# Causal attention of two heads side by side in blocks of 256 queries, with each block's division at a listed step

## What is computed

```python
q = einsum('bld,dhk->blhk', x, Wq)                # B, L, D, H, HD = 2, 2048, 256, 16, 64
latent = einsum('bld,dc->blc', x, Wkv_down)       # LD = 64
k = einsum('blc,chk->blhk', latent, Wk_up)
v = einsum('blc,chk->blhk', latent, Wv_up)
attn = einsum('bqhd,bkhd->bhqk', q, k) / sqrt(64)
attn = softmax(where(key <= query, attn, -big))
out = einsum('bhqk,bkhd->bqhd', attn, v);  return einsum('bqhd,hdo->bqo', out, Wout)
x = x + attention(layernorm(x));  x = x + experts(layernorm(x))   # ... two rounds of experts
```

## Time and profile before

| | us |
|---|---|
| median of 3 runs | 2812.95 (2809.69 to 2816.72) |
| the profiled execution | 2814.72 |
| its span, first to last instruction | 2813.0 |
| mean granted clock of TensorE | 0.968 of 2.4 GHz |
| prologue, to the first scores (L489) | 79.5 |
| 16 turns of attention | 1757.5 |
| rest (experts) | 976.0 |

### The profile page before, as it was taken

How to read it: one execution, slowest core, us unless ns; L and a number is a source line. 1 busy time by engine, 2 the same in 40 slices (tenths; PEclk the granted TensorE clock), 3 DMA queues, 4 the chain that set the end, 5 groups by cost and what they waited for, 6 DMA issues and landing times. The chain is left out here.

```text
span 2813.0 us, 47115 instructions
## 1 busy us (share of the span) xinstructions
PE 2616.8 (93%) x13460; PEld 2182.7 (78%) x13460; DVE 1971.6 (70%) x4391; ACT 1801.6 (64%) x4164; POOL 1933.0 (69%) x1735
## 2 busy tenths in 40 slices
PE   6999999999989999999999999979998998889885
PEld 4787787788777887788788788868887887769774
DVE  7788787788887777778778778445665454754456
ACT  2677777777767777777777777833324664226652
POOL 3698898898878889889889889932262232454235
PEclk8999999999999999999999999999998999879998
DMA  3011111111111111111111000154343442224553
GB/s 73 23 48 40 41 38 43 36 33 32 48 44 25 37 24 26 28 24 30 30 28 30 24 20 20 24 160 141 104 165 135 145 152 87 85 96 153 176 162 120
DMA packets 162670, 193.11 MB, mean 69 GB/s; under 512 B 57827, under 2 KB 126697, under 8 KB 161910
## 3 DMA queue, kind: packets, MB, share of 16 engines
q1 hardware_dynamic: 149110, 156.26, 19.2%
q0 software_dynamic: 12288, 33.57, 3.6%
q10 hardware_dynamic: 1024, 0.26, 0.0%
HBM read 116.02 MB, written 83.16 MB: 71 GB/s over the span
## 5 line engine op out<-in xcount | busy, mean ns | idle before, releaser
L305 POOL TENSOR_TENSOR pl<-pr,ph 128x512 fp32r<-128x512 f32 (+3 forms) x1184 | 1372.5, 1182 | 214.7 <-ACT ph L740 196.3
L737 ACT ACTIVATE pr<-ps 128x512 f32<-128x512 f32 (+3 forms) x1280 | 688.2, 538 | 410.0 <-PE ps L490 174.6
L1012 DVE TENSOR_REDUCE part<-ps 128x1 f32<-128x512 f32 (+3 forms) x1152 | 703.1, 617 | 129.8 <-PE ps L475 114.2
L740 ACT ACTIVATE ph<-ps 128x512 fp32r<-128x512 f32 (+3 forms) x1280 | 686.8, 537 | 0.0
L475 PE MATMUL ps<-k_hi,q_parts 128*128 128x512 f32 (+3 forms) x1280 | 490.5, 384 | 52.9 <-DVE part L1012 46.9
L489 PE MATMUL ps<-q_parts,k_hi 128*128 128x512 f32 (+3 forms) x1280 | 483.0, 377 | 0.2
L490 PE MATMUL ps<-q_row,k_lo 65*128 65x512 f32 (+3 forms) x1280 | 472.0, 369 | 0.0
L475 PEld LDWEIGHTS ps<-k_hi,q_parts 128*128 128x128 f32 x1280 | 243.5, 190 | 141.5 <-DVE part L1012 66.9
L489 PEld LDWEIGHTS ps<-q_parts,k_hi 128*128 128x128 f32 x1280 | 242.0, 189 | 55.3 <-ACT ph L740 7.7
L490 PEld LDWEIGHTS ps<-q_row,k_lo 65*128 65x128 f32 x1280 | 242.6, 190 | 34.3
L1660 PE MATMUL ps<-exp_up,yy 128*128 x888 | 249.2, 417 | 2.4 <-ACT yy L1833 2.2
(11 more groups left out here) (258 smaller groups left out, 4623.6 us busy)
## 6 DMA issues: line engine op xcount, KB each, us to landing
work<-x_slots SPq DMA_DIRECT2D x148, 128.0 KB, 2.2
e_slots<-work SPq DMA_DIRECT2D x148, 128.0 KB, 1.7
y_latent<-y_sums SPq DMA_DIRECT2D x128, 128.0 KB, 3.2
yg<-y_latent SPq DMA_DIRECT2D x32, 512.0 KB, 5.1
rec<-recip_rows SPq DMA_DIRECT2D x127, 128.0 KB, 3.4
x_slots<-zero_rows SPq DMA_DIRECT2D x32, 296.0 KB, 3.6
acc_shared<-accw SPq DMA_DIRECT2D x14, 512.0 KB, 3.1
accr<-acc_shared SPq DMA_DIRECT2D x12, 512.0 KB, 4.1
```

The lines of the kernel that those rows point to most:

```text
L305: eng.tensor_tensor(pl[:, s % RING, 0:w], pr[:, s % PR_RING, 0:w], f32(ph[:, s % RING, 0:w]), ALU.subtract).then_inc(sem, 1)
L737: act.activation(pr[:, s % PR_RING, 0:w], src, ACT.Exp).then_inc(S["probs"], 1)
L740: act.activation(ph[:, s % RING, 0:w], src, ACT.Exp).then_inc(S["probs_hi"], 1)
L1012: ins = dve.tensor_reduce(dst, src[:, 0:w], AX.X, ALU.max)
```

## The change

A step now holds both heads of the pair. `q_parts` and `q_row` are one tensor each, laid out by block, head and query; a block is 256 queries of both heads, 512 columns in all. There are eight blocks, `b`, of `2b + 2` steps: 72 steps a turn. Two steps of each block lie on the diagonal; the first is 512 wide, the second 256 (the later 128 queries of both heads). The mask of the scores is one operation on two times 128 columns.

The maximum pass still has 80 matmuls a turn, now spread over 72 steps (every ninth step has two), 28 ahead (`LEAD`). The keys of one are cut evenly (`even_parts`), so that five tiles of keys are three and two and not four and one. The prologue does 28 maxima and three of the four groups of casts.

DVE takes the low part of every ninth step (`s % 9 == 4`, in its step `s + 1`): eight a turn, all 512 wide. POOL has the other 64. Inversion is ten steps behind a block's end. The division has a list, `DIVIDE_AT`; modulo 72, divisions are in DVE's steps 0, 18, 20, 27, 36, 45, 54, 63, its low parts in 5, 14, 23, 32, 41, 50, 59, 68, and its casts in 2, 6, 19, 21, 29, 33, 43, 46. SP's three DMAs of a block stand at steps of their own, 7, 11 and 13 behind the block's end, and the store one behind the division. The last block's division, left to the next stage as before, is now of 128 partitions by 256.

```diff
-SCORE_STEPS = [(qb, kt) for qb in range(QB) for kt in range(TPB * (qb + 1))]
-MAX_STEPS = [(TPB * qb + j, c) for qb in range(QB) for j in range(TPB) for c in range(qb + 1)]
-INVERT_AFTER = 8
-DIVIDE_AFTER = 13
+SCORE_STEPS = [(b, kt) for b in range(NB) for kt in range(2 * b + 2)]
+MAX_STEPS = [(b, head, j, c, at * P, n * P) for b in range(NB) for head in range(2) for j in range(2)
+             for c, (at, n) in enumerate(even_parts(2 * b + j + 1))]
+LEAD = 28
+COPY_AFTER, INVERT_AFTER = 6, 10
+SUMS_AFTER, RECIP_AFTER, SPREAD_AFTER = 7, 11, 13
+DIVIDE_AT = (18, 27, 36, 45, 54, 63, 72, 92)
...
-BANK_JOBS = [(1, "row", 0, 3), (5, "row", 1, 0), (8, "proj", 2, 0), (13, "row", 1, 1), (16, "proj", 2, 1),
+BANK_JOBS = [(0, "row", 0, 3), (10, "row", 0, 4), (15, "proj", 1, 0), (21, "row", 0, 5), (27, "proj", 1, 1), (35, "row", 0, 6),
...
-ON_DVE = [s % STEPS in (10, 20, 30) for s in range(2 * STEPS)]
+ON_DVE = [s % 9 == 4 for s in range(STEPS)]
...
+def maxes_at(s, p):
+    steps = range(LEAD + MAXES * s // STEPS, LEAD + MAXES * (s + 1) // STEPS)
+    return [(p + n // MAXES, n % MAXES) for n in steps if p + n // MAXES < TURNS]
...
-                def scores(half, m, s, p, first, last):
-                    off = P * max(0, kt - TPB * qb)
+                def scores(s, p, first):
+                    b, kt = SCORE_STEPS[s]
+                    off = 0 if kt <= 2 * b else P
...
-                    pe.matmul(out, khs[p // PAIRS][:, k], qa[half][:, q], start=True, stop=False)
-                    pe.matmul(out, kls[p // PAIRS][0:LD + 1, k], qc[half][:, q], start=False, stop=True).then_inc(S["scored"], 1)
+                    pe.matmul(out, khs[p // PAIRS][:, k], qa[:, b, :, off:QW], start=True, stop=False)
+                    pe.matmul(out, kls[p // PAIRS][0:LD + 1, k], qc[:, b, :, off:QW], start=False, stop=True).then_inc(S["scored"], 1)
...
-                    dve.tensor_tensor(src, src, T["mask_kq"][:, :], ALU.add).then_inc(S["masked"], 1)
+                    dve.tensor_tensor(src, src, T["mask_kq"][:, None, :].broadcast_to([P, 2, P]), ALU.add).then_inc(S["masked"], 1)
...
-                        block_jobs(divide, s, DIVIDE_AFTER, p, first)
+                        divided_jobs(divide, s, 0, p, first)
...
+                def turn(p, first):
+                    for s in range(STEPS):
+                        block_jobs(take_sums, s, SUMS_AFTER, p, first)
+                        block_jobs(put_recip, s, RECIP_AFTER, p, first)
+                        block_jobs(spread, s, SPREAD_AFTER, p, first)
+                        divided_jobs(store, s, 1, p, first)
```

More of the change, by code:

```diff
@@ L233, in first_row_job @@
             return START_JOBS.index(("row", qb))
-        def first_max_steps(g):
-            steps = [m for m in range(STEPS) if MAX_STEPS[m][0] // TPB == g]
-            return steps[:TPB], steps[TPB:]
         def jobs_at(s, p):
@@ L430, in _ @@
                 for p in range(TURNS):
-                    turn(p, p < TURNS - 2, first=p == 0)
+                    turn(p, p == 0)
+                store(TURNS - 1, NB - 2)
                 hand_over()
@@ new lines, in _ @@
+                for n in range(16):
+                    max_scores(0, 8 + n)
+                    if n == 1:
+                        first_row(1)
+                    if n == 2:
+                        start_project(2)
+                    if n == 3:
+                        latents(2)
+                    if n == 4:
+                        turn_x(3)
+                    if n == 6:
+                        turn_latents(2)
+                    if n % 2 and n >= 5:
+                        make_m(2 + (n - 5) // 2)
+                    if n == 10:
+                        first_row(2)
+                    if n == 12:
+                        start_project(3)
+                    if n == 13:
+                        latents(3)
@@ L662, in _ @@
+                turn_latents(3)
+                make_n(0)
+                make_n(1)
+                for m in range(24, LEAD):
+                    max_scores(0, m)
+                    if m < 27:
+                        make_n(2 * (m - 24) + 2)
+                        make_n(2 * (m - 24) + 3)
                 pe.wait_ge(S["v_lo"], QB)
@@ L932, in turn, with divide @@
+                def divide(p, b):
+                    q = b % QB
+                    dve.wait_ge(S[f"recip_in{q}"], DMA * (2 * p + b // QB + 1))
+                    dve.tensor_tensor(y[0:LD, q, :], y[0:LD, q, :], rec[:, q, :], ALU.mult).then_inc(S["normed"], 1)
                 def turn(p, first, last):
-                    for s in range(2 * STEPS):
-                        half, m = s // STEPS, s % STEPS
+                    for s in range(STEPS):
                         if is_diagonal(s):
@@ L936, in turn @@
                             mask_scores(p, s)
-                        if not (last and half == 1):
-                            qb = MAX_STEPS[m][0] // TPB
-                            h2, q2 = (half + 1, qb - 2) if qb >= 2 else (half, qb + 2)
-                            made = rows_to(p, h2, q2)
-                            read_max(m, STEPS + 2 * STEPS * p + s, 8 * p + 4 * (half + 1) + qb, made)
-                        for n, (_, head, qb) in splits_at(s, last):
-                            split_hi(head % 2, qb, *split_waits(p, head, qb, first))
+                        for pair, m in maxes_at(s, p):
+                            read_max(pair, m)
@@ L945, in turn @@
+                        for _, (_, off, g, head) in splits_at(s, last):
+                            split_hi(g, head, *split_waits(p, off, g))
                         if s and ON_DVE[s - 1]:
```

571 lines of the change are left out of this document (283 added, 288 removed).

## The result

| | before | after |
|---|---|---|
| median of 9 runs each, side by side | 2814.87 | 2805.11 |
| range of the runs | 2809.69 to 2823.5 | 2799.48 to 2808.38 |
| ratio after / before | | 0.996 (95% interval 0.995 to 0.9971) |
| profiled execution, span | 2813.0 | 2806.6 |

The account below looks back on a forecast made before the run. PE was taken as the bound: 101.9 us of work a plain turn plus 7.0 waiting, nearly all for DVE's reductions. Savings of 36 (plain turns), 2, 3, 2 and 6 sum to 49; 2812.95 - 50 gave 2763 us, range 2715 to 2804.

Parts of the forecast that it names:

- The floor: PE's work in a plain turn without waits: falls 1.3 us, 101.9 to 100.6, as 128-wide step matmuls go.
- DVE's work: DVE's operations in a turn: masks 2.6 us less, low parts 3.6 more at 1.376 each, together 1 us more.
- DVE's stretches: Steps where DVE has more work than PE: PE's waits fall from 7.0 to 5.5 us a turn, bounds 2.5 and 9.
- gain stays a floor's gain: Plain turns: DVE's collisions only change partners, PE still waits 7.0 us; 25 us less, 2788; chance 0.2.
- DVE becomes the bound: Low parts beside other DVE work hold steps: 12 us of waits, a turn of 112.6, 2862 us; chance 0.1.
- the waits nearly go: Lone SBUF operations fit DVE's idle time: PE waits 2.5 us a turn, 92 us less, 2721; chance 0.2.
- Turn 6: The turn that also normalises the second sequence: 2 us off 128.9, bounds -8 and +6, jobs no closer together.
- Turn 7: The turn of 116.2 us after the normalising one: 3 us off, as a plain turn.
- Prologue: Before the first scores, 79.5 us: 12 of 40 maxima leave, 6 us off, bounds 0 and 10.
- SP's queue: SP's DMAs and stores as single steps, one tight: 0 taken, up to 0.5 us a turn from ACT's slack.

Follow-up runs that it names:

- e12: Changed kernel with inversion eight steps behind a block's end, as before, instead of ten: 2802.76 us, ratio 0.9971 to the kernel before.
- e7: Kernel before the change with inversion ten steps behind a block's end instead of eight and division 16 instead of 13: 2848.02 us, ratio 1.0002.
- e1: Changed kernel with the second maximum of a two-maxima step behind the step's scores instead of ahead: 2773.86 us, ratio 0.9876 to the kernel before.
- e11: Changed kernel with a maximum's keys cut as before, five tiles into four and one, instead of evenly: 2833.06 us, ratio 1.0068 to the kernel before.
- e3: Changed kernel with four low parts a turn on DVE instead of eight, POOL taking the others: 2791.65 us, ratio 0.9928 to the kernel before.
- e2: Changed kernel with every division in the step of a DVE low part, directly behind it: 2939.25 us, ratio 1.0457 to the kernel before.
- e9: Changed kernel with every division one step behind the step of a DVE low part: 2908.9 us, ratio 1.0337 to the kernel before.
- e8: Changed kernel with second maximum behind scores, four DVE low parts a turn, turn 6's layernorm work halved, three casts moved: 2763.77 us, ratio 0.9701 to the kernel before.
- e4: Changed kernel with the steps of two maxima moved from s % 9 == 8 to s % 9 == 3: 2818.05 us, ratio 1.0016 to the kernel before.
- e15: Changed kernel with GpSimd's low parts cut to 128 columns, leaving work out: 2728.94 us, ratio 0.9701 to the kernel before.
- e10: Changed kernel with maxima 32 ahead instead of 28, four more in the prologue: 2821.34 us, ratio 1.0026 to the kernel before.

## Why the prediction was wrong, point by point

- **The floor** (101.9 to 100.6): right, and with it 13 x 1.3 of the gain. Two runs of 128 columns cost nothing extra.
- **DVE's work**: the mask's 0.42 was right. The low part's 1.376 was not a property of the operation but of its neighbours before; it became 0.98. This term made the forecast slower and can't explain a result that is slower still.
- **DVE's stretches**, from 7.0 to 5.5 us of waits: the step that failed; they stayed at 7.1. It gained the missing 1.5 us from three things: no DMA waits, which e12 shows to be worth nothing; distances, which in the old layout are worth 0.3 us a turn at most (e7); and fewer narrow steps, which no run priced alone. Its own numbers don't give 5.5 either: the excesses of four of its five stretches are 1.0, 1.7, 1.3 and 1.2, and with half a microsecond for each of the five that is 7.7 before the fifth excess is counted. And it compared DVE's work with PE's over whole stretches, without a look at where PE meets the delay: two maxima ahead of the scores, with two banks, make the scores wait for DVE's newest reduction but one at eight places a turn. e1 prices that at 1.7 us a turn. The order printed ahead of the prediction showed the pair; I described it and gave it no term. The even cut of the keys had no term either, and e11 prices it at 2.0 us the other way. That the sum of the waits came out as before is these two nearly cancelling, with 0.7 for the added low parts (e3) beside them. As to the places it was better: the waits at 71 to 8, 35, 49 and 57 lie in or two or three steps behind four of the five stretches named; behind 17 to 23 there are only the 0.49 of step 26.
- **Rival "gain stays a floor's gain"**: right for plain turns in size (1.2 against 1.3 each), partly by luck: its reason, that collisions only change partners, has in it neither the pairs nor the even cut. Its 2788 missed turns 6 and 7 as well.
- **Rival "DVE becomes the bound"**: not this kernel, but e2 and e9 are it. Its mechanism, a low part, its neighbour and the lock of GpSimd, came to 13.6 to 15.2 us of waits where I had 12, and what kept the changed kernel from it is the division's list.
- **Rival "the waits nearly go"**: not this kernel either. The 2.5 us that it named are reached by e8 (2.6), with the pairs, four low parts and three casts moved.
- **Turn 6** (-2, with +6 as the worst): +9.5, outside my bounds. I had written that its jobs' places were "no closer together on the whole". Two of the four normalisations, steps 24 and 42, now stand right behind the low parts of 23 and 41 and ahead of the pairs of 26 and 44. Of PE's waits read step by step, 5.3 us are at step 26, 3.8 at 8, 3.2 at 44 and 2.2 at 63; the 2.3 of step 27 lie in a stretch of the lower clock. The page of waits says the same with its longest: in this turn

```profile
PEld ps L515 <- DVE part L1066: 19.2, 10, 5.3
PE ps L515 <- DVE part L1066: 17.3, 10, 4.8
```

  against, before,

```profile
PEld ps L475 <- DVE part L1012: 16.8, 13, 2.8
```

  Fewer waits and longer ones, and at the end of a long one PE's clock falls to its lower level of 1.2 GHz for a while: in this turn that happened four times, at 12.5, 50.0, 87.6 and 121.7 us from its start, each time within 1.3 us of the scores of step 8, 26, 44 or 63, with which the wait there ends. 20.5 us of the turn were granted at that level, 10.2 before, 0.93 against 0.96 in the mean; ten us more at half the clock are an estimated 5 of the 9.5 us. e1 takes 6.8 us of the turn away, e3 4.5, e4 10.3, e15 18.8, all with less time at the lower level (10.2, 13.7, 6.8 and 3.8 us). But e12, which moves only the inversions and leaves a plain turn at its length, has 134.2 us in turn 6 with 10.2 at the lower level, 4.2 less than the changed kernel. Each of these figures is one execution, so differences of 4 us in turn 6 are not shown to be the edit's.
- **Turn 7** (+4.1 against -3): e1 gives back 2.0 and e15 3.3. What the rest is was not looked into.
- **Prologue** (-6, bounds 0 and -10): -11.6. e10 puts the maxima at 4 to 8 of it, where I had 7; the term had no entry for the new order of the rest.
- **SP's queue**: the slack that I took was there; no wait of ACT for a store showed.

The miss of the sum is 43 us on the profiled spans: 20 in the plain turns, 11.5 in turn 6, 7 in turn 7, 1.6 in the last, 8 in the experts' stage, within its scatter, less 5.6 better in the prologue.

Still open: the 0.9 us at the turn's change, of which the other variants keep 0.6 to 1.0 and e4, in which step 71 has one maximum, only 0.1 (so it seems to be a late price of that pair); how the prologue's 11.6 us divide; what the fewer narrow steps gave; and for e4, e10 and e11 only the steps of the new waits were read, not a cause for each one.

## What to carry to other kernels

Where two engines are joined by two buffers and one of them works in order, count what stands behind the second use of a buffer in the same step: moving it behind the urgent work cost nothing and took the ratio from 0.996 to 0.9876, twice what the whole change gave. Compare the engines' work step by step and let the delay run along to the next such place, rather than over a stretch, and do this for the odd turn too, where lumps of other work meet the same places. An idle time that ends with a DMA was worth nothing here on an engine that idles anyway; and before work is spread or moved, ask what else holds SBUF at that time.

## What the runs showed of the hardware

With GpSimd busy 86% of a turn, a division of 64 x 512 directly behind a low part took 1.41 us, one reduction further 1.30, three steps or more away 0.95, and 0.78 with GpSimd's operations cut short. So the second of two SBUF operations in a row on VectorE is the dear one (1.77 us in the timeline of e2). What it stands behind can be read from the ends. GpSimd's row beside that pair is

```profile
1302.73 1.62 POOL L889 TENSOR_TENSOR q_parts<-q_raw,q_parts 64x512 fp32r<-64x512 f32 x1
```

It ends at 1304.35, and the division, which started at 1303.12, ends at 1304.89, 0.54 us later. This is so for every division between 980 and 1700 us of the changed kernel that starts while an operation of GpSimd runs: 47 of 53, with durations from 0.69 to 1.45 us, end 0.54 to 0.55 us after the end of that operation. The other six started with GpSimd idle and took 0.67. So the length of a division is a matter of when in GpSimd's operation it starts. It works the other way round too: the operation of GpSimd above started 0.47 us before the end of VectorE's low part and took 1.62 us, where most of its kind in e2 took 1.3. Behind a low part a division starts early in GpSimd's next operation, here 0.39 us after its start, and waits out nearly all of it. The casts, with a single input, do the same: the 49 of 55 in that stretch that start inside an operation of GpSimd end 0.28 to 0.34 us after its end, and take 0.84 us in the mean against 0.44 in e15. A normalisation of one input more than doubles (0.42 to 0.91). I had not expected either. Reductions and masks in PSUM did not stretch (a reduction took 0.684 in the changed kernel and 0.686 in e15).
